# Attention's product with the values as the stationary operand, four heads in groups of 32 columns

## What is computed

```python
tokens = layernorm(patches_in_5_shifts @ W.T + b) * gamma + beta   # 32 images, 36 patches
h = concatenate([tokens, weight[x_txt]], axis=1)                   # 32 x 68 x 192
# attention on layernorm(h): 12 heads of 16
true_scores = q @ k.T * 0.25
pred_scores = ex_quant(q) @ ex_quant(k).T       # only sign and exponent kept
idx = top_k(pred_scores, 32)
attn = zeros.at[idx].set(softmax(true_scores[idx]))
h = h + (attn @ v) @ proj_w.T + proj_b
# then 128 experts with two routed matrices each, 4 of 128 per token and side
h = h + ffn(layernorm(h))
```

## Time and profile before

| | us |
|---|---|
| median of 3 runs | 949.04 (945.45 to 955.71) |
| the profiled run | 945.62 |
| its span | 943.9 |
| PE busy in the span | 789.4 (84%) |
| DVE busy | 653.0 (69%) |
| POOL busy | 564.5 (60%) |
| ACT busy | 362.7 (38%) |

### The profile page before, as it was taken

One profiled execution on the slowest core, in us unless ns is written; L12 is line 12 of the kernel. 1 busy time (PEld: TensorE's weight loads), 2 busy tenths in 40 slices (PEclk: granted clock), 3 DMA queues, 4 the chain that ended last, 5 costly groups with the idle time before them and its releaser, 6 DMA issues.

```text
span 943.9 us, 22303 instructions
## 1 busy us (share of the span) xinstructions
PE 789.4 (84%) x6357; PEld 659.8 (70%) x6357; DVE 653.0 (69%) x4126; ACT 362.7 (38%) x1147; POOL 564.5 (60%) x788
## 2 busy tenths in 40 slices
PE   5789999999999889888874699999988799399800
PEld 3678888888888678777653477999866458356700
DVE  2198899899999799888867577666753354155433
ACT  0123444444444354535322333444422357345700
POOL 5255676676766567575468517406776677775075
PEclk9788899999999588778655599999997899799955
DMA  9322543544514233634019498756899798499533
GB/s 326 116 95 107 190 165 138 187 146 157 185 64 165 89 116 98 188 103 133 16 50 283 151 288 276 211 146 184 255 405 408 249 335 286 147 300 369 192 100 92
DMA packets 81696, 177.25 MB, mean 188 GB/s; under 512 B 12968, under 2 KB 38344, under 8 KB 78760
## 3 DMA queue, kind: packets, MB, share of 16 engines
q1 hardware_dynamic: 56200, 120.62, 38.2%
q10 hardware_dynamic: 14112, 32.12, 9.1%
q0 software_dynamic: 11264, 23.09, 8.1%
HBM read 94.25 MB, written 81.53 MB: 186 GB/s over the span
## 4 chain that ended last, share of the span: by engine, by line
PE 45%; POOL 25%; issue 11%; ACT 8%; DMA 6%; DVE 4%; SPq 1%; POOLq 0%; ACTq 0%; DVEq 0%
PE bank L1056 6%; POOL early L782 6%; PE bank L1036 5%; PE bank L1356 5%; PE bank L1304 5%; PE bank L1292 4%; PE bank L1358 3%; PE bank L1309 3%; POOL qbd L646 3%; POOL eqbd L655 3%; PE bank L1104 3%; PE bank L1346 3%; PE bank L1081 3%; POOL slots_g L789 3%; POOL slots_x L758 2%
## 5 line engine op out<-in xcount | busy, mean ns | idle before, releaser
L1441 DVE MATCH_REPLACE8 work<-top,work 128x68 f32<-128x68 f32 x896 | 179.5, 213 | 0.0
L1435 DVE MAX8 top<-work 128x8 f32<-128x68 f32 x896 | 129.7, 215 | 32.6 <-ACT tru L832 29.2
L1747 DVE COPY place<-bank 96x256 f32<-96x256 f32 x147 | 56.9, 416 | 64.3 <-PE bank L1292 62.4
L782 POOL DMA_INDIRECT early<-slots_h,s_all x68 | 65.7, 966 | 57.7 <-DMA slots_h<-m_y 37.6
L1036 PE MATMUL bank<-early,xp 128*128 128x192 f32 x432 | 92.3, 378 | 7.0 <-DMA xp<-in_a_x 5.1
L758 POOL DMA_INDIRECT slots_x<-early,s_all x68 | 68.0, 1001 | 46.8 <-DVE s_all L1633 27.2
L1036 PEld LDWEIGHTS bank<-early,xp 128*128 128x128 f32 x432 | 89.4, 231 | 9.0 <-DMA xp<-in_a_x 5.4
L782 POOL DMA_INDIRECT early<-slots_y,s_all x68 | 65.0, 955 | 50.9 <-DMA slots_y<-m_y 29.0
L1755 DVE COPY place<-bank 128x128 f32<-128x128 f32 x147 | 37.5, 287 | 81.4 <-PE bank L1346 81.1
L706 POOL TENSOR_TENSOR sc<-work,tru 128x476 f32<-128x476 f32 x32 | 38.0, 1189 | 83.3 <-ACT work L886 83.3
L789 POOL DMA_INDIRECT slots_g<-early,s_all x68 | 66.3, 976 | 27.4 <-issue 20.1
(11 more groups left out here) (202 smaller groups left out, 1896.0 us busy)
## 6 DMA issues: line engine op xcount, KB each, us to landing
early<-slots_x SPq DMA_DIRECT2D x49, 384.0 KB, 3.8
slots_y<-m_y ACTq DMA_DIRECT2D x49, 384.0 KB
slots_h<-m_y ACTq DMA_DIRECT2D x49, 256.0 KB
early<-slots_g SPq DMA_DIRECT2D x49, 256.0 KB
f_all<-in_f_know SPq DMA_DIRECT2D x16, 768.0 KB, 9.6
r_all<-in_r_know SPq DMA_DIRECT2D x16, 768.0 KB
slots_x<-zero SPq DMA_DIRECT2D x28, 360.0 KB, 3.0
slots_x<-zero SPq DMA_DIRECT2D x28, 336.0 KB, 3.3
```

The source lines that it names most:

```text
L782: nc.gpsimd.indirect_dma_start(g_in[:, i % DEPTH, k, 0:width], None, src, bass.IndirectOffsetOnAxis(s_all[:, r - 1, i, k:k + 1], 0)).then_ ...
L1435: last = nc.vector.max(top8[:, c, :], work[:, par, c, :])
L1441: last = nc.vector.match_replace(work[:, par, c, :], top8[:, c, :], work[:, par, c, :], TAKEN)
L1747: nc.vector.tensor_copy(m_xT[t][0:HALF], turn_bank[t][0:HALF, 0:2 * P].rearrange("p (c s) -> p c s", c=2)).then_inc(sem["m_xt0"], 1)
```

## The change

`attend` swaps its operands. `v[:, par, head, :]`, now 32 columns wide (16 values, 16 zeros), is the stationary operand, the turned probabilities are the moving one. Head 4c + q writes partitions 32q to 32q + 32 of `ps_o`, in columns c x 68 on; the same with 32 columns of ones as stationary operand puts the row sums on the same partitions, three blocks further. TRIO = 3, so there are 3 x 2 x 4 = 24 products in place of 12. DVE takes the reciprocal of all sums, [128, 3, 68], and multiplies [128, 3, 68] straight into `oT`, which already lies as the projection wants it. `turn_out` and ACT's copy are gone, with their semaphores `ot_mm` and `ot_copied`; `project_out` waits for `o_done` and makes three products of 128 rows. `v_cols` and `w_proj` are laid out by heads with zeros between. The memset of `v` writes 0 in place of 1.

```diff
-PT = HEADS * (HD + 1)
+TRIO = HEADS // 4
...
-        v_b = sb("v_b", [HALF, 2, P])
-        wp = sb("wp", [HALF, 2, D])
+        v_b = sb("v_b", [P, TRIO, P])
+        wp = sb("wp", [P, TRIO, D])
...
-        v = sb("v", [S, 2, HEADS, HD + 1])
-        o = sb("o", [S, D])
+        v = sb("v", [S, 2, HEADS, 32])
...
-        srec = sb("srec", [S, HEADS])
+        srec = sb("srec", [P, TRIO, S])
...
-        oT = sb("oT", [HALF, 2, S])
+        oT = sb("oT", [P, TRIO, S])
...
-                if attended:
-                    act.wait_ge(sem["ot_mm"], b - 1)
-                    if runs(b, 3, BATCH + 1):
-                        act.wait_ge(sem["proj_mm"], b - 2)
-                    nc.scalar.activation(oT[:], ps_front[0:HALF, 0:2 * S].rearrange("p (c s) -> p c s", c=2),
-                                         ACT.Copy).then_inc(sem["ot_copied"], 1)
...
-                if runs(b, 4, BATCH):
-                    pe.wait_ge(sem["ot_copied"], b - 3)
...
-                for g in range(2):
-                    for h in range(HH):
-                        head = HH * g + h
-                        last = nc.tensor.matmul(ps_o[0:S, head * (HD + 1):(head + 1) * (HD + 1)], pT[:, g, h * S:(h + 1) * S],
-                                                v[:, par, head, :], start=True, stop=True)
+                for c in range(TRIO):
+                    for stationary, at in ((None, c), (ones_f[0:S, 0:32], TRIO + c)):
+                        for q in range(4):
+                            head = 4 * c + q
+                            g, h = divmod(head, HH)
+                            last = nc.tensor.matmul(ps_o[32 * q:32 * q + 32, at * S:(at + 1) * S], v[:, par, head, :] if stationary is None else stationary,
+                                                    pT[:, g, h * S:(h + 1) * S], start=True, stop=True)
                 last.then_inc(sem["o_mm"], 1)
 
-            def turn_out(b):
-
+            def project_out(b, m):
                 pe.wait_ge(sem["o_done"], b + 1)
-                pe.wait_ge(sem["qk_copied"], b + 4 if runs(b, 0, BATCH - 4) else BATCH)
-                for c in range(2):
-                    last = nc.tensor.transpose(ps_front[0:HALF, c * S:(c + 1) * S], o[:, c * HALF:(c + 1) * HALF],
-                                               ident[0:S, 0:S])
-                last.then_inc(sem["ot_mm"], 1)
-
-            def project_out(b, m):
-                pe.wait_ge(sem["ot_copied"], b + 1)
...
-                for g in range(2):
-                    last = nc.tensor.matmul(ps_vp[0:S, D:2 * D], oT[:, g, :], wp[:, g, :], start=(g == 0), stop=(g == 1))
+                for c in range(TRIO):
+                    last = nc.tensor.matmul(ps_vp[0:S, D:2 * D], oT[:, c, :], wp[:, c, :], start=(c == 0), stop=(c == TRIO - 1))
...
-                if attended:
-                    turn_out(b - 2)
...
-            nc.vector.memset(v[:], 1.0).then_inc(sem["zeroed"], 1)
+            nc.vector.memset(v[:], 0.0).then_inc(sem["zeroed"], 1)
...
-                    attended_v = ps_o[0:S, 0:PT].rearrange("p (h c) -> p h c", h=HEADS)
                     dve.wait_ge(sem["o_mm"], b - 1)
-                    nc.vector.reciprocal(srec[:], attended_v[:, :, HD]).then_inc(sem["srec_done"], 1)
+                    nc.vector.reciprocal(srec[:], ps_o[:, TRIO * S:2 * TRIO * S].rearrange("p (c s) -> p c s", c=TRIO)).then_inc(sem["srec_done"], 1)
...
                     if runs(b, 3, BATCH + 1):
-                        dve.wait_ge(sem["ot_mm"], b - 2)
-                    nc.vector.tensor_tensor(o[:].rearrange("p (h c) -> p h c", h=HEADS), attended_v[:, :, 0:HD],
-                                            srec[:].unsqueeze(2).to_broadcast([S, HEADS, HD]), ALU.mult).then_inc(sem["o_done"], 1)
+                        dve.wait_ge(sem["proj_mm"], b - 2)
+                    nc.vector.tensor_tensor(oT[:], ps_o[:, 0:TRIO * S].rearrange("p (c s) -> p c s", c=TRIO), srec[:], ALU.mult).then_inc(sem["o_done"], 1)
```

More of the change, by code:

```diff
@@ L255, in build @@
             "topk", "dve_steps", "gap_done", "masked", "smax_done", "shifted", "exp_done", "srec_done",
-            "pt_mm", "pt_copied", "o_mm", "o_done", "ot_mm", "ot_copied", "proj_mm", "pj_done", "row_mm", "row_ready", "h1_done", "h1_out0", "h1_out1",
+            "pt_mm", "pt_copied", "o_mm", "o_done", "proj_mm", "pj_done", "row_mm", "row_ready", "h1_done", "h1_out0", "h1_out1",
             "emb_steps", "emb_ss", "emb_root", "emb_scaled", "emb_flip", "emb_ready",
@@ L1137, in _ @@
             nc.tensor.transpose(bank[5][:, 0:P], emb_s[:].rearrange("p r d -> p (r d)"), ident[:]).then_inc(sem["emb_flip"], 1)
-            for g in range(2):
-                last = nc.tensor.matmul(bank[1][:, 0:D], v_b[:, g, :], wp[:, g, :], start=(g == 0), stop=(g == 1))
+            for c in range(TRIO):
+                last = nc.tensor.matmul(bank[1][:, 0:D], v_b[:, c, :], wp[:, c, :], start=(c == 0), stop=(c == TRIO - 1))
             last.then_inc(sem["row_mm"], 1)
@@ L1859, in lay_out @@
     split = lambda m: m.reshape(2, HALF, -1).transpose(1, 0, 2)
+    by_head = lambda m: np.pad(m.reshape(TRIO, 4, HD, -1), ((0, 0), (0, 0), (0, 32 - HD), (0, 0))).reshape(TRIO, P, -1).transpose(1, 0, 2)
     return {
@@ L1865, in lay_out @@
         "row_vec": rows(L0_attn_proj_b),
-        "v_cols": np.broadcast_to(L0_attn_qkv_b[2 * D:].reshape(2, HALF).T[:, :, None], (HALF, 2, P)), "w_proj": split(L0_attn_proj_w.T),
+        "v_cols": np.broadcast_to(by_head(L0_attn_qkv_b[2 * D:, None]), (P, TRIO, P)), "w_proj": by_head(L0_attn_proj_w.T),
         "f_know": L0_ffn_f_know.reshape(NE, HALF, 2 * R).transpose(1, 0, 2), "r_know": L0_ffn_r_know.transpose(1, 0, 2),
```

## The result

The changed kernel takes **966.7 us** (median of 4 runs, 962.7 to 971.5); the kernel before took 947.4 us in 4 runs beside it. The ratio is **1.0217, 95% interval 1.018 to 1.0255**: slower by 2.2%, where 976 us (954 to 1000) was forecast. The profiled execution took 971.5 us (span 969.8), the longest of the four, against a span of 943.9 before. The chip has a slower state in which some runs fall; ratios leave these out, which here are two of the five runs of `before_long_late`, its profiled one among them.

The account below looks back on a forecast made before the run. DVE and PE were taken to be full together in the slot loop, DVE ending full-clock slots and PE low-clock ones. Terms 10.9 + 5.0 + 8.1 + 2.5 + 0.8 = 27.3 us on 949.0 gave 976 us, range 954 to 1000.

Parts of the forecast that it names:

- the ten routing slots: Second part of the slot loop, with routing beside it: +3.7, +3.4 and +1.0 us, 8.1 in all.
- attend's term: PE's attend per slot: 1.63 us at full clock, +0.19; bounds -0.5 to +1.6, far off +6.5.
- DVE's term: Reciprocal of 204 elements takes 1.42 us at 6.25 ns each; with the scaling, DVE gets +1.21 us per attended slot.
- The first 19 slots: Embedding beside attention: ten full-clock slots cost 10.9 us by DVE, nine with low clock 5.0.
- two deep: PE's attend: only two narrow records overlap at a time, so 48 records take 1.43 us, plus 0.2 for switches.
- the last three: Last three slots, chains: +1.2 reciprocal, -0.8 turn, copy and waits, +0.4 to 0.7 third product; 2.5 us, between 0 and 4.
- The reciprocal's price: Slot loop: DVE's added +1.21 us per attended slot, less the DVE idle time that takes it.
- The other edits: Attended slots: third projection product +0.33 us, transposes gone 0.12 on PE; ACT's copy gone, worth nothing in full slots.
- Start: Kernel start: larger `v_cols` and `w_proj` loads add 0.8 us, bounds 0 and 0.8.
- PE as the bound: Rival: narrow products do not overlap, attend +1.6 us, PE passes DVE in full-clock slots; 994 us, chance 0.10.
- another outcome: Rival: PE pauses and the clock falls more often, ten more low slots at +1.0 us; 986 us, chance 0.15.
- the third rival: The clock falls less often in the slot loop and DVE alone sets the pace; 954 us, chance 0.12.

Follow-up runs that it names:

- before_long_late: Kernel before plus an extra, unread 68x204 DVE reciprocal per attended slot, both reciprocals moved behind the key quantisation that issues `ek`: ratio 1.0198.
- neighbours: Changed kernel with each head's value product and sum issued next to each other in one column group: 966.8 us, 1.0231.
- short_recip: Changed kernel with DVE's reciprocal covering 12 elements instead of 204, the other factors a constant: 944.7 us, 1.0000.
- recip_late: Changed kernel with the wait for attend and the reciprocal moved behind the key quantisation that issues `ek`: 954.9 us, 1.0083.
- before_long: Kernel before plus an extra, unread 68x204 DVE reciprocal ahead of the real one, PE's work unchanged: 997.8 us, 1.0564.
- group_after_group: Changed kernel with all six attend products of one column group in a row, then the next group: 1001.6 us, 1.0613.
- act_recip: Changed kernel with the reciprocal made on ACT as exp(-ln x) instead of on DVE: 952.6 us, 1.0071.
- act_one_set: Changed kernel with the reciprocal on ACT as exp(-ln x) and one load, at ACT's start, of a table set holding both functions: 944.0 us, 0.9945.

## Why the prediction was right, and where it was wrong

The direction, the place and the cause came out as forecast; the sum was 7 to 8 us too high. The direction was earned; that the number came so near is in part luck, since two errors in the ten routing slots pull against each other: attend's term had the wrong sign, and the reciprocal's was priced by the wrong path.

- **DVE's term: right in size.** 1.42 us forecast, 1.425 measured, by the reciprocals' slope of 6.25 ns an element. By the estimate from the Trainium skill's repeat count of 8 (VectorE: DVE Perf Modes, "First, the fixed hardware budget") it would have been some 0.4 us longer; the trace does not agree, and the row decides. DVE busy 12.12 and 13.18 us in plain and normalising slots (12.1 and 13.3 forecast), idle 0.25 (0.27), `eqbd` 1.2 us later: all as written.
- **The first 19 slots: +14.1 us measured, +15.9 forecast.** The count of DVE against DVE held: sixteen of the slots end within 0.6 us of DVE's own work, though seven and not ten now have a clock of 1.00.
- **The step that failed: "two deep".** Attend was put at +0.19 us at full clock and +0.35 at the low level. Measured: -0.60 and -1.16 (2.68 to 1.52). The expert stretch alternates two groups because its operands are 64 columns wide, and I took the number of groups in use for the depth of the overlap, and took starts to follow the program's order, which `neighbours` shows they don't. The rule of the Trainium skill (TensorEngine Tiling (Array Packing), "Theoretical Speedup") that I cited and set aside was right, and the trace agrees for float32 products of two records each (0.84 us for 48 records); I had its -0.5 as the lower bound. So at the low level PE's work fell instead of growing: -1.16 for attend, +0.66 and about -0.2 for the products added and gone, an estimate of -0.7 from these rows where the forecast's own terms give +0.8. The ten routing slots came to +3.9 instead of 8.1 and the last three to +0.4 instead of 2.5: a shorter attend should also let the reciprocal start earlier, which no run shows by itself.
- **The reciprocal's price: near in size, wrong in its path.** I wrote that the paths through DVE and POOL are level "and the reciprocal stands ahead of both", and then priced the first only: DVE's length, less the idle that takes it. In the 19 full slots that is the greater part of the truth (12.1 us against `short_recip`, 8.5 of it left in `recip_late`). In the ten routing slots it isn't: of 8.3 us, 6.8 go when the reciprocal stands behind `ek`. With PE's work unchanged the error shows at full size: `before_long` costs 21.8 us in these ten slots and 53 in all, where my count came to 25. In the changed kernel PE's lighter work hides most of that.
- **The other edits: zero in sum**, by `short_recip`. The projection's third product is there as counted: six records in 1.03 us to the next, 0.17 each; the turn, the copy and their waits left no gain that can be told.
- **Start: 0.8 us can't be settled.** The third slot starts at 72.4 for 70.8, but between 69.8 and 72.8 in the profiles here, whichever size the loads have.
- **The rivals.** PE as the bound didn't come; `group_after_group` shows that it would have with the same products in another order, at 1.061. The clock was lower in the first stretch (0.88 for 0.91) and not in the second (0.78 for 0.77). Measured against `short_recip`, with the same products, it was 0.88 for 0.91 and 0.78 for 0.81, so a part of the 20 us may come by way of the clock, which I had as another outcome and not as a part of the likeliest; how large that part is stays open. The 954 us of the third rival was mis-added: its terms, +8.5, -6.5 and +5, give 956 on the median of 949.0.

## What to carry to other kernels

Price a longer instruction twice: by its engine's idle time, and by what is queued behind it that doesn't need it. Which of the two counts depends on the stage: here the length in the slots where DVE is full, the delay of `ek` in those where it has idle time. Moving the reciprocal back by one instruction, behind `ek`, returned over half. Where a change of layout replicates a small quantity (12 sums per partition to 204), look for an engine with idle time for it before giving up the layout; and keep the products that share a group of columns apart in the order of issue.

## What the runs showed of the hardware

- Four groups of 32 columns overlap for fp32 products in two records: 48 records of 68 moving columns in 0.84 us, 0.0147 each between sets, where two groups had given 0.064 for 128 moving columns. Six products of one group in a row take 2.34 us.
- Records start out of the program's order across groups: a product that waits for its own group is passed by those of others (`neighbours`, 0.91 us).
- A DVE reciprocal costs 6.25 ns an element on 68 partitions as on 128 (1.43 and 1.42 us for 204), while Ln and Exp on ACT take 0.34 and 0.37 us for the same tensor. Placed without further care the pair loads two tables, 1283 ns each, every time (64 loads in `act_recip`); with one load of the set that holds both functions at ACT's start, that one is the only load left (`act_one_set`).
- A longer reciprocal on DVE ahead of `ek` went with a lower granted clock though PE's work was the same: a mean of 0.84 fell to 0.81 in `before_long`, in each of four runs. In the ten routing slots it went with the reciprocal's place and not with its length: 0.66 ahead of `ek`, 0.78 behind it (`before_long_late`), 0.77 without it.
